# First attention: values in two passes, sums by a column of ones; exclusive recurrence over three slots; last weights early; 32 contraction rows later

## What is computed

```
x = x + attn0(wkv(x, f, f, w, u, cond))      # layer 0
x = x + ffn0 (wkv(x, ...))                   # layer 1, fp8
x = x + attn1(wkv(x, ...))                   # layer 2
x = x + ffn1 (wkv(x, ...))                   # layer 3, ternary weights

def wkv(r, k, v, w, u, time_emb):            # per channel, along the 256 tokens
    # forward and backward scans  a = a*decay + ek*v,  b = b*decay + ek,  each including its own token
    num = nf + nb - ekv + euk * vf
    den = df + db - ek + euk                 # euk = exp(min(u + k, 30)), ek = exp(min(k, 30))
    return sigmoid(r) * (num / max(den, 1e-8)) * (0.8 + 0.2 * tf)

def attn0(x, W, g1, g2, g3):                 # 16 heads of width 16; w = x @ W.T
    q, k, v = rms_norm(w, g1), rms_norm(w, g2), rms_norm(w, g3)
    att = q @ k.T / 4
    score = softmax(att, axis=-1) + softmax(att, axis=-2)
    return (score @ v) @ W

def bitlinear(x, w):                         # ffn1 = bitlinear(relu(bitlinear(x, w1))**2, w2)
    w_scale = 1 / clip(mean(abs(w)), EPS);  w_q = clip(round(w * w_scale), -1, 1) / w_scale
```

## Time and profile before

| | |
|---|---|
| median of 2 runs | 465.86 us (465.75 to 465.96) |
| span of the profiled execution | 465.9 us |
| PE / DVE / ACT / POOL busy | 278.0 / 316.4 / 189.0 / 50.3 us |
| PE weight loads busy | 164.8 us |
| HBM read, written | 6.16 MB, 1.05 MB |

### The profile page before, as it was taken

How to read it: one execution, slowest core, us unless ns; L and a number is a source line. 1 busy time by engine, 2 the same in 40 slices (tenths; PEclk the granted TensorE clock), 3 DMA queues, 4 the chain that set the end, 5 groups by cost and what they waited for, 6 DMA issues and landing times.

```text
span 465.9 us, 4913 instructions
## 1 busy us (share of the span) xinstructions
PE 278.0 (60%) x1766; PEld 164.8 (35%) x1766; DVE 316.4 (68%) x549; ACT 189.0 (41%) x308; POOL 50.3 (11%) x77
## 2 busy tenths in 40 slices
PE   0214334553655284453448677798889999865754
PEld 0212111231322042131224344564666756533522
DVE  4989999999999899991575564434456323187562
ACT  5534335356554636431320232531743533224322
POOL 4010121112111201211202021102000000000000
PEclk9956655665595555666667776958975565676987
DMA  7000444444444444584000000000000000000010
GB/s 247 12 0 4 88 91 90 90 91 90 91 136 90 91 91 91 97 213 97 0 0 0 1 0 0 1 1 1 1 2 0 1 0 1 0 0 2 34 35 23
DMA packets 8088, 22.20 MB, mean 48 GB/s; under 512 B 1537, under 2 KB 2945, under 8 KB 7681
## 3 DMA queue, kind: packets, MB, share of 16 engines
q0 software_dynamic: 4032, 14.68, 16.8%
q1 hardware_dynamic: 4032, 7.21, 4.6%
HBM read 6.16 MB, written 1.05 MB: 15 GB/s over the span
## 4 chain that ended last, share of the span: by engine, by line
DVE 40%; PE 36%; issue 9%; ACT 7%; DMA 6%; POOL 1%; DVEq 0%; ACTq 0%; POOLq 0%
PE PS L1121 8%; DVE fwd L609 6%; DVE bwd L615 6%; PE PM L1069 5%; DVE rsum L708 5%; PE PO L1139 4%; PE PM L1018 4%; DMA fwd<-bwd 4%; PE PM L966 4%; PE PO L1001 2%; DVE mid L598 2%; DMA fwd<-mid 2%; DVE fwd L876 2%; DVE G L584 1%; PE PO L1203 1%
## 5 line engine op out<-in xcount | busy, mean ns | idle before, releaser
L810 DVE TENSOR_REDUCE kp<-PS 128x2 f32<-128x256 f32 x64 | 32.2, 552 | 34.1 <-PE PS L1100 34.1
L523 ACT ACTIVATE E<-PS 128x384 f32<-128x384 f32 x64 | 28.0, 491 | 43.3 <-PE PS L1121 43.1
L461 ACT ACTIVATE E<-PS,negc,escale 128x1024 f32<-128x1024 f32 x32 | 38.0, 1193 | 16.8 <-PE PS L980 16.8
L993 PE MATMUL PO<-E,vt 128*32 128x256 f32 x256 | 30.1, 618 | 21.7 <-DVE ytok L735 11.7
L1001 PE MATMUL PO<-ident,yc 128*128 128x128 f32 x64 | 19.7, 406 | 38.1 <-ACT yc L445 38.1
L386 ACT ACTIVATE fwd<-fwd,lnmin 128x512 f32<-128x512 f32 x16 | 11.6, 722 | 75.0 <-DMA fwd<-bwd 71.4
L708 DVE TENSOR_REDUCE rsum<-E 128x4 f32<-128x1024 f32 x32 | 38.1, 1203 | 0.0
L980 PE MATMUL PS<-TP 32*128 32x256 f16 x256 | 24.6, 370 | 22.4 <-ACT E L461 16.3
L966 PE MATMUL PM<-ident,kp 128*128 128x128 f32 x128 | 24.5, 354 | 9.8 <-DVE kp L651 5.7
L1121 PE MATMUL PS<-TP 19*128 19x128 f32 (+1 forms) x128 | 24.1, 488 | 5.4 <-ACT E L523 3.2
L1069 PE MATMUL PM<-G,sg 128*128 128x512 f32 x32 | 23.7, 909 | 4.5 <-DVE sg L638 4.5
(11 more groups left out here) (156 smaller groups left out, 609.7 us busy)
## 6 DMA issues: line engine op xcount, KB each, us to landing
fwd<-mid POOLq DMA_DIRECT2D x14, 512.0 KB, 4.5
fwd<-bwd POOLq DMA_DIRECT2D x14, 512.0 KB, 4.5
kT<-in_kT SPq DMA_DIRECT2D x4, 256.0 KB, 4.6
xT<-in_xT SPq DMA_DIRECT2D x4, 256.0 KB, 6.2
G<-in_attn SPq DMA_DIRECT2D x1, 1024.0 KB, 4.8
ek<-in_w SPq DMA_DIRECT2D x1, 1024.0 KB, 6.0
ekv<-in_w SPq DMA_DIRECT2D x1, 1024.0 KB, 10.5
out<-mid SPq DMA_DIRECT2D x8, 128.0 KB, 1.7
```

Source lines behind the costliest of these rows:

```text
L461: nc.scalar.activation(E[:, p % 4], PS[:, 2 * (p % 2):2 * (p % 2) + 2, :], ACT.Exp, bias=negc[:], scale=escale[:]).then_inc(S["e0_done"], 1)
L523: nc.scalar.activation(E[:, p % 4, i, 0:384], PS[:, i, 0:384], ACT.Exp, scale=QSCALE).then_inc(S["e1_done"], 1)
L810: nc.vector.tensor_reduce(kp[:, b % 2, u * H + 2 * j:u * H + 2 * j + 2, D], PS[:, at0:at0 + 2, lo:hi], AX, ALU.max, negate=True).then_inc( ...
L993: ins = nc.tensor.matmul(PO[SLOT * g:SLOT * (g + 1), q % 2, 0:T], vt[:, b % 2, v * H + 4 * c + g, :], E[:, (2 * q + g // 2) % 4, g % 2, v ...
```

## The change

Four things are done together.

**First attention.** The reduction over E is gone. `vt` carries a column of ones beside v, so that `values0` gives E v and the row sums in one pass. After the turn DVE takes the reciprocals from PSUM (`links`), writes v over the sums into a new tile `vr`, and scales the turned rows into `ytok`. A second pass, `columns0`, multiplies `vr` with E and leaves its result already turned; ACT copies it (`turned_copy`), and `project_both` adds it through a second, permuted copy of the output weights (`w0p`). E has six buffers, and a slot's values stand one slot earlier.

```
-            def values0(q):   # waits vcols_done; banks q % 2, E of 4
+            def values0(q):
+                pe.wait_ge(S["e0_done"], 2 * q + 2)
+                ... 8 matmuls PO[.., 0, 0:T] <- vt (v and ones), E[:, (2 * q + g // 2) % 6, ..]
+            def columns0(q):
+                at = q // 2 % 2 * T
+                pe.wait_ge(S["vcols_done"], q + 1)
+                ...
+                for v in range(TT):
+                    for g in range(4):
+                        ins = nc.tensor.matmul(PO[SLOT * g:SLOT * (g + 1), 1, at:at + T], vr[:, q % 2, v * 4 + g, :],
+                                               E[:, (2 * q + g // 2) % 6, g % 2, v * T:(v + 1) * T],
+                                               start=(q % 2 == 0 and v == 0), stop=(q % 2 == 1 and v == TT - 1),
+                                               skip_group_check=True)
+                ins.then_inc(S["pv2_done"], 1)
+            def project_both(b):
+                pe.wait_ge(S["yT0_done"], b + 1)
+                ...
+                for n, (w, k, src) in enumerate(((w0[:, 1], 0, yT), (w0[:, 1], 1, yT), (w0p, 0, yB), (w0p, 1, yB))):
+                    ...
+                    for o in range(HALF):
+                        ins = nc.tensor.matmul(PM[:, 1, o * T:(o + 1) * T], w[:, k, o * P:(o + 1) * P], src[:, k, :], ...)
+                ins.then_inc(S["out0_done"], 1)
```

```
-                ins = nc.vector.tensor_reduce(rsum[:, q % 2, 2 * (p % 2):2 * (p % 2) + 2, :],
-                                              E[:, p % 4].rearrange("p i (v t) -> p i v t", v=TT), AX, ALU.add)
+            def links(q):
+                dve.wait_ge(S["turned0_done"], q + 1)
+                link(nc.vector.reciprocal(rec, rows[:, :, :, D]))
+                ...
+                nc.vector.tensor_tensor(dst, src, rec[:, :, :, None].broadcast_to([P, TT, 4, D]),
+                                        ALU.mult).then_inc(S["vcols_done"], 1)
+                ...
+                nc.vector.tensor_tensor(ytok[...], rows[:, :, :, 0:D], rec[...], ALU.mult).then_inc(S["y0_done"], 1)
```

```
-        WKV0 = {(16 * i) // 7: EARLY + i for i in range(LAYERS * B - EARLY)}
+        M_AT = {n: 3 * (n - RAMP) for n in range(RAMP, LAYERS * B)}
-                nc.vector.scalar_tensor_tensor(mid[:, r, 0], mid[:, r, 0], EXP30, ek[:, seg(b)], ALU.min, ALU.subtract)
+                nc.vector.tensor_scalar(mid[:, n % 2, 0], mid[:, n % 2, 0], EXP30, None, ALU.min)
-                nc.vector.tensor_tensor_scan(bwd[:, r, i][:, ::-1], DT[n % 2][:, 1:SEG + 1][:, ::-1],
-                                             src[:, seg(b)][:, ::-1], 0.0, ALU.mult, ALU.add)
+                nc.vector.tensor_tensor_scan(bwd[:, n % 2, i, 0:SEG - 1][:, ::-1], src[:, seg(b, 1, SEG - 1)][:, ::-1],
+                                             DT[n % 2][:, 1:SEG][:, ::-1], 0.0, ALU.add, ALU.mult)
+            square0(0)            # ACT, ahead of the loop
+            weight_abs(0)
+            rms(0)
+            weight_abs(1)
+            act.wait_ge(S["gains_done"], 1)
+            wkv(1)                # waits for the DMA that adds bwd of recurrence 1
+            kT_copy(0)
```

```
-            ROWS = D + 1 + TT
+            ROWS = SLOT
```

## The result

The changed kernel takes 416.74 us (median of two runs, 414.29 and 419.19) against 465.86: 0.893 of the time, 95% interval 0.880 to 0.907, 49 us less. The forecast was 404, with an own range of 394 to 414 and 386 to 437 with the nearest rivals.

A forecast was written before the change was run, and what follows sets the result against it. DVE was taken to bound the first loop and PE attn1's; after the change PE would carry more in the first. 465.9 - 47.6 (attn1's projection earlier) - 2 + 1 - 13 = 404.3; forecast 404 us, own range 394 to 414.

The forecast's parts named there:

- the clock of attn1 does not move: Rival for attn1's loop: the rows change nothing, the first loop's gain stays, 417 us; chance 0.20.
- 126 us of PE at clock 0.59: First loop: PE's work up to the last `ytok`, with the second pass and doubled output projection, more than DVE's 109.
- I add 4 us: First loop: addition to PE's load for places where DVE is the longer one, giving 130 us.
- DVE bounds the loop at a high clock: Rival for the first loop: 109 us and little waiting, total 375, or 387 with half the clock's gain; chance 0.09.
- The slower rival: First loop: the new cycle runs in line, 15 us per group, 528 us; chance 0.08, including partly eaten gains.
- the signs named ahead: Profile: first E at 41 us, PE busier than DVE, `links` 8 us apart, attn1's clock above 0.8 or at 0.67.
- the three signs of a wrong forecast: First loop: `links` and PE waiting for each other, backward scans over 1.3 us, ACT's added-DMA waits near 5 us each.
- The ramp: Before the first scores: `kT_copy(0)` waits behind recurrence 1's added DMA, moving first scores from 36.3 to 41.2 us.
- Behind the loop: Last `ytok` to attn1's projection: 26 us instead of 23, with longer projection, four table loads and two backward scans.
- rows -13: Attn1's loop: 32 contraction rows keep PE's clock high for longer, -13 us, lower value of -13 to -19.
- ternary steps -2: Attn1: roundings and ternary steps leave ACT and DVE; only ACT's 2 x 2.03 us could have held up PE, -2.
- the two slow stretches: Attn1's loop before, 350 to 377 and 380.5 to 404.2: PE busy without a gap at clock 0.50.

The follow-up runs named there:

- experiment 9: Changed kernel with the 32 sums over E put back on DVE at their old place, result unused; 440.50 us, ratio 0.948.
- experiment 5: Changed kernel with half of the second pass over E left out (4 matmuls instead of 8 per group); 413.93 us, ratio 0.887.
- experiment 6: Changed kernel with the backward scans of recurrences 4 to 14 cut to half their length; 416.94 us, ratio 0.896.
- experiment 12: Changed kernel with the 32 unused sums over E back on DVE and only 40 of 128 second-pass matmuls left; 432.75 us, ratio 0.935.
- experiment 10: Changed kernel with `links` moved ahead of the recurrence's steps in the same slot on DVE; 421.95 us, ratio 0.908.
- experiment 4: Changed kernel with batch 0's `kT_copy` ahead of recurrence 1's Ln and Exp in ACT's order; 413.31 us, ratio 0.890.
- experiment 11: Changed kernel with `kT_copy`, `low_parts`, `turned_copy`, POOL's memset and the last backward scans moved, and one table load for recurrences 13 and 14; 402.25 us, ratio 0.862.
- experiment 2: Changed kernel with 19 instead of 32 contraction rows in attn1's scores and maxima; 422.87 us, ratio 0.909.
- experiment 3: Kernel before with 32 instead of 19 contraction rows in attn1's scores and maxima; 455.65 us against 462.54, ratio 0.983.
- experiment 7: Changed kernel with the next batch's `kT_copy` and `low_parts` one slot earlier in the first loop; 409.98 us, ratio 0.883.
- experiment 1: Changed kernel unaltered, run again beside the kernel before; median of six 414.74 us, ratio 0.893.
- experiment 8: Changed kernel with one table load for Ln and Exp ahead of recurrences 13 and 14 instead of four; 418.08 us, ratio 0.898.

## Why the prediction was right, and where it was not

The time lies inside the range of 386 to 437, but not inside the forecast's own 394 to 414. It comes within a us of a rival, "the clock of attn1 does not move" (417), whose mechanism the runs exclude: that agreement is chance, and the number alone would have pointed at the wrong cause.

**What bounds the kernel** was read rightly: the first loop was DVE's, and taking work from it there shortened it. DVE's new load was put at 109 us up to the last `ytok` and measured 109.1; its largest term, 36.2 us for the sums, measured 33.6 (experiment 9), so other terms were off by as much the other way.

**The first loop**, 130 forecast and 134.1 measured, is near for a wrong reason. The step that failed is "126 us of PE at clock 0.59": the granted clock was 0.76 to 0.84 in every version of the changed loop, and PE was busy for 93.5 us, close to the 85 us that the prediction gave for a stretch all at 2.4 GHz. The term "I add 4 us" for the interlocking was the other error, with the opposite sign: waits are 40.7 us. The one is 32.5 us less than forecast, the other 36.7 more, and that they nearly cancel is luck. So the loop was forecast as PE-bound at a low clock, and it is a cycle of waits with PE's work on it (experiment 5) and the length of DVE's backward scans not (experiment 6); with DVE loaded to 92%, both engines' work counts (experiments 9 and 12). The rival "DVE bounds the loop at a high clock, 109 us and little waiting" was nearer on the clock and wrong on the waiting. The slower rival named the mechanism that is there, `links` behind a pair of scans: PE waits 16.4 us for it. A group takes 8.4 us, far from that rival's 15; experiment 10 shows that the scans are no pure loss there, since without them in front of `links` DVE waits 14.0 us for the turned rows.

Of the signs named ahead, PE was not busier than DVE (93.5 and 109.1 us), and the two passes took 46.1 us where 60 or 35 were named. None of the three signs of a wrong forecast came: DVE waits 1.8 us in all for the turned rows, the backward scans have means of 1.21 and 1.28 us, and ACT waits four times for the added DMAs, 8.2 us in all. They did not cover the way in which the forecast of the loop was wrong.

The page "TensorEngine Tiling (Array Packing)" of the Trainium skill (section Key Properties) says that a change of the tiling mode drains the engine. The prediction made 5 us of it with a price of its own, the 0.33 us before the first weight load of the values, and misread that row: the idle time is that of the weight loads, and PE is in its transposes meanwhile, until 218.09. Between two loads of the same mode the weight loads are idle for 0.23 us as well:

```profile
217.40 0.69 PE L1001 MATMUL PO<-ident,yc 128*128 128x128 f32 x2 [6.60 <-ACT yc L445]
...
218.45 0.20 PEld L993 LDWEIGHTS PO<-E,vt 128*32 128x32 f32 x4 [0.23 <-issue]
```

In the changed kernel PE's view of lines closes to 134.2 of 134.1 us with busy time and waits for other engines alone, so this trace leaves no such term apart; if there is one, it lies inside what is counted as busy.

**The ramp**, 41.2 forecast and 42.6 measured: the mechanism (`kT_copy(0)` behind a DMA) is as told, and experiment 4 gives 4.7 us back. What was missed lies earlier: DVE's norm of the first projection, `kp`, starts 1.9 us later than before (28.72 and 26.83), and POOL's with it. Of that, 1.0 us stands ahead of the first gate. ACT waits 0.86, 0.90 and 0.94 us for the later parts of `kT` in front of three exponentials; its Ln of recurrence 0 starts at 17.27, and DVE waits 3.04 us for it and makes the gate (L613) at 18.69 instead of 17.65. The other 0.85 us are DVE's own: from that gate to `kp` pass 10.03 us instead of 9.18, since four scans (of recurrence 2) stand in between where two stood. The DMA is issued at 31.61, where the forecast had 29.85.

**Behind the loop**, 26 forecast and 27.4 measured. The four table loads are there, 1.28 us each, and what I had not seen is the bias add that takes 2.60 instead of 0.60 us while POOL's memset runs. The page "GPSIMD Engine Reference" of the Trainium skill (section Specifications) says that GpSimd's interfaces to SBUF are shared with VectorE, with contention for instructions in a mode that uses two ports or with two inputs from there; this trace agrees that DVE is slowed beside POOL, by those 2.0 us, and in experiment 11, with the memset elsewhere, they are gone. In which mode the bias add ran it does not show.

**Attn1.** -15 forecast (rows -13, ternary steps -2), -13.4 in the profile. Experiments 2 and 3 show that the rows raise the clock, with 12 us in the one profile of experiment 3; by the medians they are worth 8.1 and 6.9 us. So the term was right in kind and, by the medians, too large by 5 to 6 us: this is the second term that was mis-sized. It was calibrated on the profiled execution of the kernel before, whose span was 465.9 while its runs beside the experiments have medians of 462.5 to 466.0. The rival that the clock does not move is ruled out. One support of the argument was misread: the output projection between the two slow stretches (L1018, from 374.55 on) was not at a high clock but for its end, since the granted clock was 0.50 up to 377 and 0.96 in the microsecond after.

**The sum.** Ramp +1.4, loop +4.1, behind it +1.4, attn1 +1.6, end -0.3: 8.2 us between 404.3 and the span of 412.5. The median is another 4.3 us above that span. Of these, 1.8 us are the difference between the time of an execution and its span (414.29 and 412.5), a term that the prediction took as nothing: "the span equals the median" compared two different things. The other 2.4 us lie between the profiled execution and the median of two, 416.74; no profile shows where.

## What to carry to other kernels

When a reduction leaves the busiest engine, look for the next limit in the waits between the engines, not in their busy shares: here 8.5 us taken from a PE at 70% shorten the loop by 5.5, and 10 us taken from a DVE at 81% by 0.3. Forecast the loop's parts and not only its length, since two errors can cancel in the sum. A move in an in-order queue is worth trying where the same wait stands at each batch change, but count what then waits instead (11 us removed, 2 arrived), and do not move the instruction that fills another engine's latency. Judge such edits by the length of their own stage, since a stage whose clock varies can hide 5 us in the total.

## What was not expected of the hardware

- *With zero rows added the granted clock was higher.* The loop of attn1 with the same matmuls took 120.8 us at 0.66 (changed kernel, in its longest execution) and 117.6 at 0.67 (before) with 19 contraction rows in the scores and maxima, and 100.0 at 0.86 to 111.2 at 0.73 with 32. Both groups have the same columns and the same instructions.
- *With 32 rows the clock still differs from profile to profile.* 100.0 (0.86), 102.7 (0.83), 104.2 (0.79), 106.3 (0.79), 108.6 (0.77), 111.2 (0.73): six runs (experiments 7, 1, the changed kernel's own, 4, 8 and 5) that don't differ in this loop, only in what stands ahead of it or not at all. They differ by up to 11 us. Whether that comes from the edits ahead of the loop or only from one execution to the next is not shown: of the six executions of the one kernel of experiment 1, four lie between 411.7 and 415.8 us and two above 418.
- *The backward scan in the order add, then multiply* takes 1.21 us for 511 elements, as long as the forward one (1.22 for 512; both are means on `ek` in the first loop, on `ekv` they are 1.28 and 1.29).
- *A bf16 TENSOR_SCALAR on DVE beside a POOL memset* takes 2.60 us for two instead of 0.60; the ramp shows the same for an operation on two SBUF tiles beside POOL's product (1.65 instead of 0.75 us, L623 at 30.35), and the kernel before has it too (L625 at 28.75, 1.65 instead of 0.69).
